# Fused two-layer decoder on one Trainium2 core: small-engine order between down products, own memory for two tiles of each down stage, four late weight slots

## The reference

```python
# the fourth block: linear attention, then a gated feed-forward with 4-bit weights and LoRA
g, u = _lin_lora(x1, ...), _lin_lora(x1, ...)      # 512 -> 1792
h = jax.nn.silu(g) * u
d = _lin_lora(h, ...)                               # 1792 -> 512
x = _layernorm(x1 + d + ...)
# the fifth: softmax attention of each tile over its context
scores = (Q @ K.T) * scale; attn = softmax(scores); x = _layernorm(x + attn @ features)
# the sixth: a gated feed-forward with weights of -1, 0, 1 and one scale for each row
gate_out = x_flat @ (gate_t * gate_s[:, None]).T    # 512 -> 1792
up_out = x_flat @ (up_t * up_s[:, None]).T
out = (silu(gate_out) * up_out) @ (down_t * down_s[:, None]).T   # 1792 -> 512
x = _layernorm(x + out)
```

## Time and profile before

| what | value |
|---|---|
| median of the runs | 727.25 us |
| the profiled execution's own time | 729.04 us |
| span of its profile | 727.2 us |
| TensorE (PE) busy | 674.2 us, 93% |
| VectorE (DVE) busy | 390.1 us, 54% |
| ScalarE (ACT) busy | 373.8 us, 51% |
| GpSimd (POOL) busy | 58.6 us, 8% |
| share of TensorE in the chain that ended last | 80% |
| mean granted TensorE clock | 0.97 |

### The profile page before, as it was taken

One profiled execution on the slowest core, in us unless ns is written; L12 is line 12 of the kernel. 1 busy time (PEld: TensorE's weight loads), 2 busy tenths in 40 slices (PEclk: granted clock), 3 DMA queues, 4 the chain that ended last, 5 costly groups with the idle time before them and its releaser, 6 DMA issues.

```text
span 727.2 us, 8509 instructions
## 1 busy us (share of the span) xinstructions
PE 674.2 (93%) x3228; PEld 471.3 (65%) x3228; DVE 390.1 (54%) x666; ACT 373.8 (51%) x502; POOL 58.6 (8%) x114
## 2 busy tenths in 40 slices
PE   6779999999998789999999999997888999999986
PEld 3445355444544348787878788885666788888864
DVE  3367777668556776565656525334654322224366
ACT  4456688856646428757575514323434433335432
POOL 1022214201120000000000000000111000000002
PEclk9989999999998899999999999999988999999999
DMA  5573097342224212232322003007201223220002
GB/s 157 199 262 115 1 295 204 108 112 78 59 61 123 59 32 91 81 104 80 105 81 76 1 0 117 1 0 317 74 1 29 54 63 84 61 59 0 1 16 100
DMA packets 24502, 62.97 MB, mean 87 GB/s; under 512 B 5477, under 2 KB 9637, under 8 KB 23566
## 3 DMA queue, kind: packets, MB, share of 16 engines
q1 hardware_dynamic: 24462, 62.43, 27.3%
HBM read 57.68 MB, written 4.73 MB: 86 GB/s over the span
## 4 chain that ended last, share of the span: by engine, by line
PE 80%; DVE 6%; ACT 6%; DMA 4%; issue 2%; POOL 1%; SPq 1%; POOLq 0%; DVEq 0%; ACTq 0%
PE bank L909 17%; PE bank L896 7%; PE bank L996 7%; PE bank L898 7%; PE bank L897 7%; PE bank L997 7%; PE bank L764 4%; PE bank L694 3%; PE bank L544 2%; PE bank L805 2%; PE bank L860 2%; PE bank L792 2%; PE bank L644 2%; DMA arena<-in_wq 1%; PE bank L756 1%
## 5 line engine op out<-in xcount | busy, mean ns | idle before, releaser
L1076 ACT ACTIVATE line<-line 128x1024 f32<-128x1024 f32 x87 | 91.0, 1046 | 0.1
L996 PE MATMUL bank<-xh,wh 128*128 128x512 f32 x224 | 87.4, 390 | 1.5 <-DVE xl L1542 1.5
L896 PE MATMUL bank<-xh,wh 128*128 128x512 f32 x224 | 88.7, 396 | 0.0
L898 PE MATMUL bank<-xh,wl 128*128 128x512 f32 x224 | 87.3, 390 | 0.0
L997 PE MATMUL bank<-xl,wh 128*128 128x512 f32 x224 | 87.2, 389 | 0.0
L897 PE MATMUL bank<-xl,wh 128*128 128x512 f32 x224 | 87.2, 389 | 0.0
L909 PE MATMUL bank<-wh,xh 128*128 128x512 f32 x208 | 83.8, 403 | 2.2 <-DVE wl L1802 1.1
L909 PE MATMUL bank<-wh,xl 128*128 128x512 f32 x208 | 82.4, 396 | 0.0
L1870 DVE SCALAR_TENSOR_TENSOR arena<-bank,ff_s,arena 128x512 f32<-128x512 f32 x28 | 20.9, 750 | 74.0 <-PE bank L997 72.7
L1790 DVE TENSOR_TENSOR xl<-arena,xh 128x1024 fp32r<-128x1024 f32 (+1 forms) x28 | 32.1, 1147 | 49.1 <-ACT xh L1303 49.1
L1303 ACT ACTIVATE xh<-arena 128x1024 fp32r<-128x1024 f32 (+1 forms) x28 | 27.7, 996 | 54.8 <-PE bank L909 48.3
(11 more groups left out here) (186 smaller groups left out, 1152.8 us busy)
## 6 DMA issues: line engine op xcount, KB each, us to landing
codes<-in_c_gu SPq DMA_DIRECT2D x14, 512.0 KB, 5.0
scales<-in_s_gu SPq DMA_DIRECT2D x28, 256.0 KB, 3.9
codes<-in_t_gu SPq DMA_DIRECT2D x14, 512.0 KB, 3.7
codes<-in_c_dn SPq DMA_DIRECT2D x7, 512.0 KB, 5.3
scales<-in_s_dn SPq DMA_DIRECT2D x14, 256.0 KB, 4.3
fold<-in_t_dn SPq DMA_DIRECT2D x1, 3584.0 KB, 16.4
codes<-in_c_qkv SPq DMA_DIRECT2D x6, 512.0 KB, 4.6
arena<-in_xT SPq DMA_DIRECT2D x4, 512.0 KB, 5.4
```

The costliest lines, as they stand in the source:

```text
L896: pe.matmul(dst, wh[:, s, c:c + P], xh[:, k, cols], start=(k == 0), stop=False)
L898: last = pe.matmul(dst, wl[:, s, c:c + P], xh[:, k, cols], start=False, stop=(k == KD - 1))
L996: pe.matmul(dst, wh[:, s, c:c + P], xh[:, k, cols], start=(k == 0), stop=False)
L1076: nc.scalar.activation(below(slot), below(slot), ACT.Prelu, bias=bias, scale=scale, alpha=alpha).then_inc(bent, 1)
```

## The change

1. **Order between down products.** On GpSimd `rstd_of` for block n-2 now follows `x2_rstd_of(n)` in step n; before, that of block n-3 did. On VectorE the steps of an iteration go x2_stats(n), x_add(n-2), x2_shift(n), x_max(n-1), stats(n-2), x3_low(n-3), where x_max(n-1) and x2_shift(n) stood ahead of x_add(n-2). The steps after the last block are written out: the first four gate and up pairs of the last feed-forward are taken apart and laid between the small products, and silus and casts likewise.
2. **Memory of their own.** `KEPT = 2`: tiles 12 and 13 of each down stage don't use the ring. They are prepared behind tile 5 and ahead of tile 6 (`IN_ORDER` is 0 to 5, 12, 13, 6 to 11). In the first stage both their hidden parts and their weights lie in `late_hidden`.
3. **Four late weight slots.** The codes of gate and up of the last feed-forward have four slots (two in `codes`, two in `scales`) and their casts four (two in `wh`, two in `wl`). The load of `ds` moves behind the fifth of them.
4. The banks of the last down stage move on by four (`t_d_bank`).

The core of the diff:

```diff
 SLOTS = 4
+KEPT = 2
 DN_LAST, T_LAST = NF - 4, NF - 6
+IN_ORDER = (*range(NF - 8), *range(NF - KEPT, NF), *range(NF - 8, NF - KEPT))
 FF_BANK = (2, 3, 7)
 PAIR_BANK = (0, 4, 6)
 FOLD_BANK = (4, 5, 7)
...
+            def place(j):
+
+                return IN_ORDER.index(j)
...
-            return 2 * tg + j if j < 2 else TG * j + tg
+            return SLOTS * tg + j if j < SLOTS else TG * j + tg
...
             sp.wait_ge(dn_wlow, NF)
             sp.dma_start(t_dn, i["t_dn"]).then_inc(in_tdn, 16)
-            sp.wait_ge(joined, JOINS * C_END)
-            sp.dma_start(ds, i["ds"].partition_broadcast(P)).then_inc(in_ds, 16)
             sp.wait_ge(bent, BENDS * C_END)
-            for n in range(0, NF // 2):
-                for s in range(2):
-                    j = 2 * n + s
-                    if j >= 2:
-                        sp.wait_ge(t_cast, j - 1)
-                    sp.dma_start(codes[:, s, :],
-                                 i["t_gu"][slice(j, j + 1), :, :].rearrange("o p c -> (o p) c")).then_inc(in_tgu[s], 16)
-                    if j >= 2:
-                        sp.wait_ge(t_h, 4 + t_place(j - 2, 1) + 1)
-                    sp.dma_start(ff_s[:, s, :], i["ts_gu"][slice(j, j + 1), :, :].rearrange("o p c -> (o p) c")).then_inc(in_ts[s], 16)
+            sp.wait_ge(scaled, C_END)
+            for j in range(NF):
+                if j >= SLOTS:
+                    sp.wait_ge(t_cast, j - SLOTS + 1)
+                sp.dma_start(t_code(j), i["t_gu"][slice(j, j + 1), :, :].rearrange("o p c -> (o p) c")).then_inc(in_tgu[j % SLOTS], 16)
+                if j >= SLOTS:
+                    sp.wait_ge(t_h, 4 + t_place(j - SLOTS, 1) + 1)
+                sp.dma_start(ff_s[:, j % SLOTS, :], i["ts_gu"][slice(j, j + 1), :, :].rearrange("o p c -> (o p) c")).then_inc(in_ts[j % SLOTS], 16)
+                if j == SLOTS:
+                    sp.wait_ge(d_ps, NT)
+                    sp.dma_start(ds, i["ds"].partition_broadcast(P)).then_inc(in_ds, 16)
...
-            for n in range(NT + 4):
+            for n in range(NT + 1):
                 if n < NT:
                     x2_stats_of(n)
-                if 1 <= n <= NT:
-                    x_max_of(n - 1)
+                if n >= 2:
+                    x_add(n - 2)
                 if n < NT:
                     x2_shift(n)
-                if 2 <= n < NT + 2:
-                    x_add(n - 2)
+                if n >= 1:
+                    x_max_of(n - 1)
+                if n >= 2:
                     stats_of(3 * NT + n - 2)
...
+            t_gate(0, 0)
+            x_probT(NT - 2)
+            x2_T(NT - 1)
+            t_up(0, 0)
+            x_out(NT - 2)
+            x_scores(NT - 1)
+            x3_T(NT - 3)
+            t_gate(1, 0)
+            x_probT(NT - 1)
+            t_up(1, 0)
+            x_out(NT - 1)
+            x3_T(NT - 2)
+            t_gate(2, 0)
+            t_up(2, 0)
+            t_gate(3, 0)
+            x3_T(NT - 1)
+            t_up(3, 0)
...
-            for j in range(1, NF):
+            for j in IN_ORDER[1:]:
                 act.wait_ge(h_ready, TG * (j + 1) + 4)
-                if j >= SLOTS:
+                if SLOTS <= j < NF - KEPT:
                     act.wait_ge(hu_used, j - SLOTS + 1)
...
+                if n == NT - 1:
                     act.wait_ge(d_ps, NT)
+                    for j in range(2):
+                        t_gu_cast(j)
+                x2_norm(n)
...
+            x_prob_out(NT - 2)
+            x2_T_out(NT - 1)
+            norm_tail(4 * NT - 3)
+            for j in range(2, SLOTS):
+                t_gu_cast(j)
+            x_exp_of(NT - 1)
+            x3_T_out(NT - 3)
+            x_prob_out(NT - 1)
             silu_table()
...
+            t_silu(0, 0)
+            norm_tail(4 * NT - 2)
+            x3_T_out(NT - 2)
+            t_silu(1, 0)
+            t_silu(2, 0)
+            norm_tail(4 * NT - 1)
...
-            for n in range(NT + 3):
+            for n in range(NT + 2):
                 if n < NT:
                     x2_rstd_of(n)
-                if n >= 3:
-                    rstd_of(3 * NT + n - 3)
+                if n >= 2:
+                    rstd_of(3 * NT + n - 2)
```

More of the change, by code:

```diff
@@ L903, in _, with down_products @@
                     gu_tile(s, 2 * n + s)
[L906 removed]
+            def down_products(dst, b, hiddens, weights, first, last):
                 for p, (h, w) in enumerate(zip(hiddens, weights)):
[L909 removed]
+                    ins = pe.matmul(dst, h[:, b * P:(b + 1) * P], w, start=first and p == 0, stop=last and p == len(hiddens) - 1)
                 return ins
             def dn_products(j, b):
[L914 to L915 removed]
+                h, l, wh_j, wl_j = hidden_part(xh, j), hidden_part(xl, j), dn_part(wh, j), dn_part(wl, j)
+                return down_products(late_bank(b)[:, :], b, (h, h, l), (wh_j, wl_j, wh_j), j == 0, j == NF - 1)
             def dn_landed(j):
                 pe.wait_ge(dn_low, down_ready(j))
[L920 removed]
+                pe.wait_ge(dn_wlow, place(j) + 1)
             def dn_group(j):
@@ L1000, in _, with t_gate, t_up @@
+            def t_gate(j, tg):
+                p = t_place(j, tg)
+                pe.wait_ge(t_cast, j + 1)
+                if p >= 6:
+                    pe.wait_ge(t_h, p + 1)
+                elif p in (2, 3):
+                    pe.wait_ge(t_h, p + 3)
+                if j == 0:
+                    pe.wait_ge(xl_ready, NT + (tg + 1) * NT // 2)
+                t_gu_part_of(j, tg, 0, t_gate_ps)
+            def t_up(j, tg):
+                t_gu_part_of(j, tg, 1, t_up_ps)
             half = DN_LAST + (NF - DN_LAST) // 2
-            for n in range(NT + 3):
-                if n < NT:
-                    dn_block(n, range(DN_LAST, half))
-                if 2 <= n < NT + 2:
+            for n in range(NT):
+                dn_block(n, range(DN_LAST, half))
+                if n >= 2:
@@ L1325, in _, with t_gu_cast @@
                 dn_weight_hi(j)
-            def t_gu_cast(s, n, free):
-                act.wait_ge(in_tgu[s], 16 * (n + 1))
-                if free is not None:
-                    act.wait_ge(t_up_ps, free)
-                nc.scalar.activation(wh[:, s, :], codes[:, s, :], ACT.Copy).then_inc(t_cast, 1)
+            def t_gu_cast(j):
+                act.wait_ge(in_tgu[j % SLOTS], 16 * (j // SLOTS + 1))
+                if j >= SLOTS:
+                    act.wait_ge(t_up_ps, t_place(j - SLOTS, 1) + 1)
+                nc.scalar.activation(t_gu_part(j), t_code(j), ACT.Copy).then_inc(t_cast, 1)
             def x2_norm(b):
@@ new lines, in x2_T_out, with x3_T_out @@
+            def x2_T_out(b):
+                x_T_out(b, late_index(b), xT, x2_ps, x2_ready)
+            def x3_T_out(b):
+                x_T_out(4 * NT + b, late_index(b), xh)
+            for n in range(NT):
+                if n >= 2:
+                    x_prob_out(n - 2)
+                if n >= 1:
+                    x2_T_out(n - 1)
+                if n >= 3:
+                    norm_tail(3 * NT + n - 3)
+                if n == NT - 1:
+                    act.wait_ge(d_ps, NT)
+                    for j in range(2):
+                        t_gu_cast(j)
+                x2_norm(n)
+                if n >= 1:
+                    x_exp_of(n - 1)
+                if n >= 3:
+                    x3_T_out(n - 3)
@@ new lines, in _ @@
+            norm_tail(4 * NT - 2)
[3 more added lines that the diff above has]
+            norm_tail(4 * NT - 1)
+            x3_T_out(NT - 1)
+            t_silu(3, 0)
+            for j in range(SLOTS):
+                t_silu(j, 1)
+                t_gu_cast(j + SLOTS)
+            for j in range(SLOTS, NF - 1):
+                for tg in range(TG):
+                    t_silu(j, tg)
+                if j + SLOTS < NF:
+                    t_gu_cast(j + SLOTS)
@@ L1388, in t_weight @@
             def t_weight(j):
[L1390 to L1393 removed]
+                nc.scalar.activation(t_dn_part(j), t_dn[:, j, :], ACT.Copy).then_inc(t_dw, 1)
             t_silu(NF - 1, 0)
@@ L1870, in t_hidden @@
                 nc.vector.scalar_tensor_tensor(h, t_bank(j, tg, 1), ff_s[:, s, 1:2], h, ALU.mult, ALU.mult).then_inc(t_h, 1)
-            for tg in range(TG):
-                for j in range(2):
-                    t_hidden(j, tg)
-            for j in range(2, NF - 1):
+            t_hidden(0, 0)
+            x_add(NT - 1)
+            stats_of(4 * NT - 1)
+            t_hidden(1, 0)
+            x3_low(NT - 2)
+            t_hidden(2, 0)
+            x3_low(NT - 1)
+            t_hidden(3, 0)
+            for j in range(SLOTS):
+                t_hidden(j, 1)
+            for j in range(SLOTS, NF - 1):
                 for tg in range(TG):
```

178 lines of the change are left out of this document (74 added, 104 removed).

## The result

The changed kernel takes 705.92 us (median of four runs, 705.0 to 708.94) against 727.13 for the kernel before; the ratio is 0.972, with a 95% interval of 0.9661 to 0.9779. The gain is 21.2 us; the forecast was 709.5 with a range of 704 to 716.

The account below looks back on a forecast made before the run. TensorE holds 80% of the chain, so gains lie in its waits and slow clock between down stages. Terms sum to 18.8 us: profiled execution 729.04 to 710.2, median 708.5, set at 709.5; range 704 to 716.

Parts of the forecast that it names:

- F: Interleaved stage's end: gate and up products fill TensorE's waits; 3.8 waits less 0.9 new plus 1.6 clock, 4.5 us saved.
- G: Second down stage: two late_hidden waits go (1.1 us), plus half the clock loss (0.9); 2.0 us saved, 1.1 to 2.8.
- D: Interleaved stage, GpSimd's order: four waits of 1.58 us of the third transpose for ScalarE's norm go, 6.3 us saved.
- E: Clock within the interleaved stage: two falls of 1.6 us go with the waits, 3.2 us saved; other bound 0.
- R2: Rival, interleaved loop closes: handovers cost 0.9 more, five periods 0.7 longer each, 3.5 us lost: 713; chance 0.09.
- B: First exponent: with the shift ahead of the maximum, norm and table load come earlier; 1.5 us of TensorE's wait saved.
- C: Second of the three exponent waits, 0.2 us, has the same cause as B and goes.
- A: First down stage: tiles 12 and 13 in own memory remove the wait for VectorE's low weight, 1.1 us saved.
- R3: Rival, everything at its best (B 1.6, F 5.9, G 2.8): 21.1 us saved, 706; chance 0.11.
- R1: Rival: clock falls as often as before, only waits are won; 13.1 us saved, 714 to 716; chance 0.14.
- R4: Rival: TensorE stays at 1.2 GHz through the interleaved stage, 746; chance 0.04 with any other gain-eating new wait.
- H: Four weight slots and the move of ds: counted at nothing, no TensorE wait for a code tile expected.

Follow-up runs that it names:

- e1: Kernel before with GpSimd's new order alone (rstd_of for block n-2 behind x2_rstd_of(n)): 717.50 us.
- e2: Changed kernel with GpSimd's old order alone (rstd_of for block n-3 behind x2_rstd_of(n)): 718.30 us.
- e3: Changed kernel with VectorE's old order of maximum, shift and x_add: 707.22 us.
- e5: Changed kernel with tiles 12 and 13 in their own memory but prepared last, behind tile 11: 709.01 us.
- e4: Changed kernel with the last blocks' small products in one row on TensorE, gate and up pairs behind them: 710.69 us.
- e7: Changed kernel with nine pauses of about 1.5 us put into the last feed-forward, where only full products run: 723.89 us.
- e10: Changed kernel with GpSimd's old order and two unused float32 products in each of the five waits: 715.86 us.

## Why the prediction was right, and where it was off

The time lay inside the range and on the side that was forecast, 3.6 us below the number. The stretches give each term its measure, in all 22.15 us against the 18.8 of the sum. F is off by 1.3, G by 1.0, the others by less than 0.5 each. The last 1.0 of the forecast was set aside because some runs of the kernel before should have fewer falls of the clock. Their mean clocks do differ: beside e1 the fastest, 723.27, has 0.975 and the slowest, 730.55, has 0.968. But where such a difference can be seen in a trace, among the changed kernels, it lies ahead of the first down stage, which the change leaves alone; that it lowers the gain isn't shown.

**D and E held** (9.71 for 9.5). The cause was where the prediction put it, in one place of GpSimd's list; e1 and e2 show it from both sides. The next thing to be late was nothing. The exponent's 0.2 us in hand were mis-sized, though on the safe side: it was put at 4.3 and is done at 3.94, because the shift, behind `x_add` as counted, starts at 2.6 and not at 2.9, and norm and exponent take 1.2 and not 1.3. TensorE takes it at 4.47, as predicted (4.5). That is 0.5 in hand, and just what VectorE's old order takes (e3). R2 fell with that.

**B and C held** (2.16 for 1.7). The table load went along with the norm. The drain of 1.38 us that the Trainium skill adds to a load ("ScalarE: Activation LUTs", What ACT_TABLE_LOAD costs), by which B would have been 0.3, is not in this trace: the norm's row ends at 499.03, the load starts at 499.05, and the exponent comes 1.30 us after the load's start.

**A held in kind**: memory, not order, is what the first stage needed (e5). It measured 1.37.

**Three sizes of the sum were wrong**, none of the places.

G's clock term was halved "with a shorter pause", where all of it came. The remaining wait of 1.1 us alone was followed by no fall in any kernel that had it; the fall came with the two further waits (e5). With the whole 1.7 G would have been 2.8, the upper bound that stood there; it measured 2.99.

F's new waits were set at 0.9, and one of 0.4 came. Its place was right, block 6's third transpose behind the silu table. That is 0.5 of the 1.3; e4, which undoes F's order, lost 5.24 for 3.1 more of waits and 1.7 by the clock (0.79 over 8 us), so 0.4 more is what no row shows, and another 0.4 stays open. The upper bound of 5.9 that stood beside F, and with it R3, had no ground in its parts: 3.8 of waits and 1.6 of clock are 5.4. That the 5.79 lies under it is luck.

A took its wait at the idle time of its row, 1.1, and got 1.37. Between full products the row is too short: a product's row ends 0.39 us after its start while the next would start after 0.227, so 0.16 of the pause lies under the row before it, and the first product behind a pause holds the second up by another 0.08. The longest pause of e7:

```profile
641.93 0.39 PE L1007 MATMUL bank<-xh,wl 128*128 128x512 f32 x1
642.15 0.39 PE L1008 MATMUL bank<-xl,wl 128*128 128x512 f32 x1
644.38 0.47 PE L1007 MATMUL bank<-xh,wh 128*128 128x512 f32 x1 [1.84 <-DVE arena L1942]
644.69 0.40 PE L1008 MATMUL bank<-xl,wh 128*128 128x512 f32 x1
```

From 642.15 to 644.69 are 2.54 us for two products that would take 0.45: 2.09 against the 1.84 of the row. A's difference is 0.27. In front of a transpose there is no such surcharge: the interleaved period shrank by 1.64 for a row of 1.58.

**R1 fell**: with the pauses gone, the clock of the changed kernel is 1.00 from 488 us to TensorE's last product, the falls came back with the pauses (e2), and went when they were filled (e10). In e1, where the five pauses are gone, one fall was left in this stage, and it came behind a new pause of 1.25 us. The rule of the Trainium skill that speaks of long pauses only ("TensorE: Matmul & The Clock Gate", HAM oscillation) doesn't cover this case; pauses of 1.6 us were enough, though not each time. **R4** had nothing for it: 1.00 over the whole stage.

**H held**: no wait for a load or a code tile came. That four slots are needed for the stage's end, where four tiles are multiplied with the first half of the rows before any slot comes free, follows from the order; a kernel with two slots and this order was not tried. The 1.85 us that the profiled execution gained before the first down stage are chance.

## What to carry to other kernels

When an engine waits at the same step in every turn of a software pipeline, look at the lists of the small engines before the long work: an operation whose input was ready a turn ago may stand behind one that waits for this turn, and moving it one turn is free. Fill what is left of the matrix engine's pauses with work that is due anyway; a pause is paid twice, by its length and at times by the clock. And compare stretches between the same events rather than totals: here they agree to 0.1 us, while the total moves by several.

## What the runs showed of the hardware beyond what I expected

- Products of no use made the stage faster: 31.75 us with two plain float32 products in each pause, 34.38 with the pauses empty (e10, e2).
- Pauses of nearly the same length had different results: in the stage of full products one fall in nine pauses of 1.5 to 1.8 us (e7), in the interleaved stage three falls in five of 1.6 (e2). Each of these falls cost 1.6 us. What decides which pause it is wasn't settled.
- A pause between full products costs TensorE about 0.25 us more than the idle time that its row shows (A, e7).
- A table load on ScalarE starts as soon as the instruction before it is done, ahead of the data that its exponent waits for (the load at 499.05, the maximum at 499.79), so it can be hidden by moving what stands in front of it.
- Before the first down stage the same code took 435.05 to 440.51 us, and the three longest of these executions had 6.8 us more at 1.2 GHz than the others. At half the clock that makes an estimated 3.4 us of the difference.
